# Moving pieces between the 32 steps of a hand-ordered scan loop

## The chip, the cores and the metric

The kernel runs on one core of a Trainium2 chip. The metric is the device time of one execution in microseconds (us), as the median over several executions. Engines are named as in the profile: PE is TensorE (PEld its weight loads), DVE is VectorE, ACT is ScalarE, POOL is GpSimd, and SP is SyncE, which here only issues DMAs.

## The reference, cut to what matters

A batch of 32 sequences of 64 tokens with 512 features passes a conditioning matmul, a Mamba block, an adapter mix and a mixture of experts. The change is within the Mamba part and what is woven into it:

```python
h0 = cond(x, subjects)                    # per-sequence 64x64 matmul + bias
xz = h0 @ in_proj_w.T;  x_, z = split(xz) # 1024 channels each
xc = silu(conv1d(x_, 4 taps))
dt_r, B, C = split(xc @ x_proj_w.T)       # rank 128, 16 states
delta = softplus(dt_r @ dt_proj_w.T + bias)
for t:                                    # 16 states per channel
    h = h * exp(delta_t * A) + (delta_t * xc_t) * B_t
    y_t = (h * C_t).sum(states)
y = (y + xc * D) * silu(z)
x1 = x + y @ out_proj_w.T
x2 = x1 @ W.T + adapters(x1)              # then x1 + experts(x2)
```

## The kernel before, in words

The 2048 tokens are cut into four blocks of 512 (8 sequences each), j = 0 to 3. A block is worked in 32 steps, m = 0 to 31: two halves of the 1024 channels, times 16 states n. Everything is float32. One step treats one state of one half, as four tiles i of 128 channels by 512 tokens:

- ACT makes the decays, `decay` (L927), one 128x504 exponential a tile, into two PSUM buffers.
- POOL makes the inflows, `inflow` (L1194), one product a tile into `dbx`. There is a single `dbx` buffer for each i, so the inflow of step m+1 for tile i has to wait for the scan of step m for tile i.
- DVE runs the recurrence along the tokens, `scan` (L1078), one instruction a tile.
- PE turns the states, `turn_h` (L716), in four tiles t of four 128x128 transposes each, into three PSUM banks. DVE then adds them, weighted with C, into `yacc`, in `add_state` (L1090). It does so one step later, two adds after every two scans. In the first step of a half (n = 0) the sum is started on ACT (L935) instead.

All other work of the layer is cut into named *pieces*, and the list `LINE` says, for each of the 32 steps, which pieces PE issues before it turns tiles 0 to 2 of that step (the first list, "firsts" below) and which between tiles 0 to 2 and tile 3 (the second list, "rests" below). Because the three banks of the transposes are reused, tile 2 of a step cannot be turned before the last add of the step before it, and tile 3 not before the first add of its own step. So the rests of step m run on PE during DVE's step m+1.

The pieces are: `cond` (conditioning, for the next block), `x` and `z` (four 128x512 matmuls each), `silu` and `zsilu` (activation of four tiles of xc or zs, on ACT), `rank` and `bc` (two halves each), `ct` (turns C), `dt` and `ln` (softplus in two parts), `turn` (turns the sums back, halves 0 and 1), `gate` (a product with silu(z) on POOL, one a tile, L1170), `out` (output projection; `out` 2i and 2i+1 fill one bank together), `xr` (turns x1 back), `xa` (adapters), `w` (mixing matmul with one more matmul for the adapter), `row` (turns x2 back), `lg` (router logits), `pre` (first half of the output projection, in the last block only) and `skip` (xc times D). `x`, `cond`, `silu`, `rank`, `bc`, `ct`, `dt0` to `dt3` and `ln0` to `ln3` work for the next block, and are left out in the last one; `out`, `xr`, `xa`, `w`, `row`, `lg`, `turn1` and `gate4` to `gate7` finish the block before, and are left out in block 0.

Every other engine takes its order from the same list:

- ACT empties the banks of step m's pieces in step m+1: firsts after decay i=1, rests after decay i=3. Decay i of a step waits for the scan two tiles earlier.
- DVE does the three convolution instructions of an `x` piece (L981) at the end of step m+1, and the mask product of `xa` (`masked`, L1033) at the end of step m itself, ahead of the convolutions.
- POOL does, after the four inflows of step m, the gates of step m-1, the finish of `ln` of step m-3 (two operations, L1159 and L1162), and the first part of `ln` of step m-2 (two operations, L1152 and L1154).
- SP issues in step m: the row of B for that step (`load_b`, into `b_all`, once POOL has finished the inflows of step m-2), then the weight tiles that take over the slots of the pieces of step m-2 (each waits until the bank of that piece is full), then stores of x1, x2T and x2 rows for pieces two steps back, each waiting for ACT. Near the end of the last block it also loads `res` again, four steps after `xr3`.

PE has only two banks for all pieces but the transposes, used in turn. So a piece waits for the emptying of the last piece but one. The lines that matter most:

```python
for piece in first_at(j, m): piece_of("body", j, piece)
turn_h(j, m, range(0, TURNED))      # TURNED = 3
for piece in rest_at(j, m): piece_of("body", j, piece)
turn_h(j, m, range(TURNED, TB))     # TB = 4
```

Of the kernel before, what the change touches and what calls it, by code (L numbers as in the profile page):

```python
# [41 lines left out]


LINE = [
    (["turn1", "gate4", "gate5"], []),
    (["gate6", "z0"], ["cond0", "gate7"]),
    (["out0"], []),
    (["out1"], ["dt4"]),
    (["out2"], []),
    (["out3"], ["ln4", "cond1"]),  # L50
    (["out4"], []),
    (["out5"], ["dt5"]),
    (["cond2"], ["ln5", "z1"]),
    (["dt6"], ["dt7", "cond3"]),
    (["ln6", "out6"], []),
    (["out7"], []),
    (["xr0", "x0"], ["skip0", "ln7"]),
    (["x1", "z2"], []),
    (["skip1", "xa", "x2"], ["xr1", "xr2"]),
    (["x3"], ["skip2", "skip3"]),  # L60
    (["turn0"], ["x4"]),
    (["silu0"], ["x5", "z3"]),
    (["x6"], ["zsilu0", "x7"]),
    (["w0", "silu1", "rank0"], []),
    (["rank1", "xr3"], ["dt0", "gate0"]),
    (["w1"], ["gate1"]),
    (["gate2", "w2"], ["ln0"]),
    (["w3", "gate3"], ["row0", "dt1"]),
    (["pre0", "bc0"], ["ln1"]),
    (["z4"], ["bc1", "pre1"]),  # L70
    ([], ["lg"]),
    (["dt2"], ["ln2", "pre2", "row1"]),
    (["z5"], ["dt3"]),
    (["z6", "row2"], ["row3"]),
    (["ln3", "pre3", "ct"], ["z7", "zsilu1"]),
    ([], []),
]
ROWS = BATCH + 2 * BB
# [2145 lines left out]
```

How the kernel before makes its waits and increments, by code:

```python
            def load_b(j, m):  # L374
                if m == 0:
                    sp.wait_ge(bt_stored, 16 * (j + 1))
                sp.wait_ge(dbx_made, j * SCANS + HT * (m + 1))
                row = bt_d[bass.ds(j, 1), m % NST, :]
                sp.dma_start(b_all[:, m % RING, :], row.broadcast_to([P, BLK])).then_inc(b_full[m % RING], 16)
# [1 line left out]
            def load_tile(n):  # L382
                section, j, piece = STREAM[n]
                name, i = name_and_number(piece)
                if n >= SLOTS:
                    sp.wait_ge(bank_full, Place(*STREAM[n - SLOTS]).full + 1)
                if name == "x":
                    tile = in_wT[:, :, i * P:(i + 1) * P]
                elif name == "z":
                    tile = in_wT[:, :, DIN + i * P:DIN + (i + 1) * P]
                elif name == "out":
                    tile = out_wT[:, i % 2 * HT:i % 2 * HT + HT, i // 2 * P:(i // 2 + 1) * P]
                elif name in ("pre", "post"):
                    tile = out_wT[:, (HT if name == "post" else 0):(DT if name == "post" else HT), i * P:(i + 1) * P]
                elif name == "xa":
                    tile = mix_d["a_T"]
                else:
                    tile = mix_d["w_T"][:, :, i * P:(i + 1) * P]
                sp.dma_start(wt[:, n % SLOTS], tile).then_inc(wt_full[n % SLOTS], 16)
# [1 line left out]
            def load_res(j):  # L401
                sp.wait_ge(first_x1_stored, 16 * (j - 1))
                sp.wait_ge(x1_stored, 16 * (TB - 1) * (j - 1))
```

## Time and profile before

| | us |
|---|---|
| median of 3 runs | 1880.04 (1879.41 to 1880.5) |
| the profiled execution | 1879.41 |
| its span, first to last instruction | 1877.6 |
| before the loop | 77.5 |
| the four blocks, 77.5 to 1069 | 991.5 |
| what follows | 808.6 |
| DVE busy in the four blocks | 967.1 |
| POOL busy in the four blocks | 806.9 |
| PE busy in the four blocks | 811.4 |

The profiled execution lasted 1879.41 us, 1.8 more than its span. A sum of terms is made against 1879.4. The adds of the last step run on for some microseconds after 1069, and what follows it (output projection of the last half, experts) is not touched by the change.

### The profile page before, as it was taken

Reading aid. Unit: us, or ns where it says so; the run is one execution under the profiler, and the core shown is the slowest. Engines: PE = TensorE matmul, PEld = TensorE weight load, DVE = VectorE, ACT = ScalarE, POOL = GpSimd, SP = SyncE. Lnnn points to the kernel's source line nnn. Section 1 sums busy time; section 2 is a strip of 40 time slices with the busy share of each in tenths; the row PEclk is TensorE's granted clock in tenths of the full one; section 3 lists DMA queues with packets and bytes.
Section 4 is the critical chain, followed back from the end, with each engine's and each line's share of the span. In section 5 each row is a group of like instructions: output and inputs, shape, how many; then the busy total and the mean of one; then the engine's idle time right before and its main releaser. Section 6 shows DMA issues by size and latency. Waiting matters only on the chain. (4 is left out here: it accounts for less than half of the span.)

```text
span 1877.6 us, 28500 instructions
## 1 busy us (share of the span) xinstructions
PE 1646.6 (88%) x7932; PEld 1211.5 (65%) x7932; DVE 1457.8 (78%) x1948; ACT 818.9 (44%) x1220; POOL 1060.1 (56%) x825
## 2 busy tenths in 40 slices
PE   8667868888998998878778999999979999999998
PEld 5255434554455554455445647778879999999997
DVE  3699999999999999999999826677346566565654
ACT  2656665566766667665664411000022233232322
POOL 0289579887599794898977470000044444344433
PEclk9869889999998999989988999999989999999999
DMA  5122112133322322222223342111155656665664
GB/s 128 38 59 68 57 41 76 60 93 81 79 96 85 90 90 68 91 90 62 74 73 112 113 165 70 67 68 44 61 138 127 175 130 172 164 135 141 155 175 70
DMA packets 129895, 182.20 MB, mean 97 GB/s; under 512 B 21379, under 2 KB 79491, under 8 KB 126660
## 3 DMA queue, kind: packets, MB, share of 16 engines
q1 hardware_dynamic: 109540, 131.85, 21.8%
q0 software_dynamic: 17760, 44.05, 12.0%
q10 hardware_dynamic: 2432, 4.33, 0.9%
q8 instruction: 77, 1.26, 0.3%
q14 instruction: 86, 0.70, 0.1%
HBM read 276.45 MB, written 37.36 MB: 167 GB/s over the span
## 5 line engine op out<-in xcount | busy, mean ns | idle before, releaser
L1194 POOL TENSOR_TENSOR arena_kept<-arena_kept,b_all 128x512 f32<-128x512 f32 x512 | 637.0, 1274 | 251.1 <-DVE arena_kept L1078 134.6
L1078 DVE TENSOR_TENSOR_SCAN arena_kept<-da,arena_kept 128x512 f32<-128x512 f32 x512 | 598.5, 1207 | 13.1 <-ACT da L927 8.1
L927 ACT ACTIVATE da<-arena_kept,a_neg 128x504 f32<-128x504 f32 x512 | 347.4, 684 | 244.6 <-DVE arena_kept L1078 238.6
L716 PE MATMUL hT<-ident_kept,arena_kept 128*128 128x128 f32 x2048 | 314.0, 300 | 145.1 <-DVE yacc L1090 88.6
L716 PEld LDWEIGHTS hT<-ident_kept,arena_kept 128*128 128x128 f32 x2048 | 256.4, 154 | 248.2 <-DVE arena_kept L1078 171.6
L1090 DVE SCALAR_TENSOR_TENSOR yacc<-hT,c_now,yacc 128x512 f32<-128x512 f32 x480 | 332.0, 735 | 4.4 <-PE hT L716 4.1
L2078 POOL DMA_INDIRECT out<-y,slots_kept x76 | 139.1, 1831 | 243.3 <-issue 174.4
L516 PE MATMUL bank<-hid,wt 128*128 128x512 f32 x512 | 239.9, 617 | 0.7 <-ACT hid L752 0.7
L516 PEld LDWEIGHTS bank<-hid,wt 128*128 128x128 f32 x512 | 98.8, 202 | 107.3 <-issue 105.7
L1946 ACT ACTIVATE gs<-egp 128x352 f32<-128x352 f32 x73 | 33.8, 464 | 237.5 <-PE eup L1278 236.9
L1714 POOL DMA_DIRECT2D slots_kept<-lists_kept x1 | 0.6, 554 | 222.7 <-DVE lists_kept L1664 222.7
L2073 POOL DMA_INDIRECT xg_kept<-x_scratch,slots_kept x72 | 74.7, 1037 | 68.8 <-ACT y L1985 39.1
L2026 DVE TENSOR_TENSOR a<-gs,eup 128x352 f32<-128x352 f32 x73 | 37.8, 518 | 93.8 <-ACT gs L1946 93.8
L1276 PE MATMUL egp<-w_up_hi_kept,xT_hi 128*128 x292 | 101.0, 346 | 2.9 <-DVE w_up_lo_kept L1270 2.9
L1552 ACT ACTIVATE sgs<-gp 128x512 f32<-128x512 f32 x24 | 14.4, 598 | 196.1 <-PE gp L1278 196.1
L1266 DVE CAST aT_hi<-aT_ps 128x256 fp32r<-128x256 f32 (+1 forms) x144 | 44.4, 350 | 68.4 <-PE aT_ps L1903 68.4
L1277 PE MATMUL egp<-w_up_lo_kept,xT_hi 128*128 x292 | 95.1, 326 | 0.0
L1278 PE MATMUL egp<-w_up_hi_kept,xT_lo 128*128 x292 | 94.8, 325 | 0.0
L1277 PE MATMUL eup<-w_up_lo_kept,xT_hi 128*128 x292 | 94.2, 322 | 0.0
L1276 PE MATMUL eup<-w_up_hi_kept,xT_hi 128*128 x292 | 94.1, 322 | 0.0
L1278 PE MATMUL eup<-w_up_hi_kept,xT_lo 128*128 x292 | 94.1, 322 | 0.0
L1985 ACT ACTIVATE y<-eyp,slots_kept 128x512 f32<-128x512 f32 x72 | 49.5, 687 | 95.6 <-PE eyp L1278 95.6
(234 smaller groups left out, 3186.9 us busy)
## 6 DMA issues: line engine op xcount, KB each, us to landing
w_up_kept<-in_up_T SPq DMA_DIRECT2D x76, 1408.0 KB, 6.1
w_dn_kept<-in_dn_T SPq DMA_DIRECT2D x76, 768.0 KB, 7.4
b_all<-bt_scratch SPq DMA_DIRECT2D x128, 256.0 KB, 3.4
wt<-in_in_T SPq DMA_DIRECT2D x64, 256.0 KB, 3.0
wt<-in_out_T SPq DMA_DIRECT2D x32, 256.0 KB, 2.9
res<-in_x_pad SPq DMA_DIRECT2D x16, 256.0 KB, 3.6
x_scratch<-res SPq DMA_DIRECT2D x16, 256.0 KB, 2.1
wt<-in_w_T SPq DMA_DIRECT2D x16, 256.0 KB, 3.0
```

The costliest lines, as they stand in the source:

```text
L516: mm = nc.tensor.matmul(bank[:], w[:, k, :], hid[:, at.block % RING, k, :], start=(k == 0), stop=(k == KM - 1))
L716: mm = nc.tensor.transpose(turned_in(j, m, t)[:, d * P:(d + 1) * P], h[:, m % RING, d, t * P:(t + 1) * P], ident[:])
L927: nc.scalar.activation(out[:, :, 1:], rows[:, :, 1:], ACT.Exp, scale=a_neg[:, d, n:n + 1]) \
L1078: nc.vector.tensor_tensor_scan(h[:, n % RING, i, :], da[i % RING][:], dbx[:, i, :], 0.0, ALU.mult, ALU.add).then_inc(scan_done, 1)
L1090: nc.vector.scalar_tensor_tensor(out=yacc[:, t, :], in0=turned_in(j, m, t)[:], scalar=scalar, in1=yacc[:, t, :], op0=ALU.mult, op1=ALU.add ...
L1194: nc.gpsimd.tensor_tensor(dbx[:, i, :], u[:, d, :], b_all[:, m % RING, :], ALU.mult) \
L1276: nc.tensor.matmul(out, lhs_hi, rhs_hi, start=first, stop=False)
L1277: nc.tensor.matmul(out, lhs_hi, rhs_lo, start=False, stop=False)
L1278: return nc.tensor.matmul(out, lhs_lo, rhs_hi, start=False, stop=last)
L1985: nc.scalar.mul(y[:, r % YS, :], yp[r % RING][:], slots[:, r, 1:2].bitcast(F32)).then_inc(y_out, 1)
L2073: nc.gpsimd.indirect_dma_start(out=xg[:, s, :], out_offset=None, in_=x2_d, in_offset=bass.IndirectOffsetOnAxis(ap=slots[:, r, 0:1], axis=0)) \
L2078: nc.gpsimd.indirect_dma_start(out=out_d, out_offset=bass.IndirectOffsetOnAxis(ap=slots[:, r % LISTS, 0:1], axis=0), in_=y[:, r % YS, :], ...
```

## The change

Only the list `LINE` changes: the same pieces, each once, stand at other steps or in the other of the two lists. No instruction is added or removed on a compute engine.

```diff
 LINE = [
-    (["turn1", "gate4", "gate5"], []),
-    (["gate6", "z0"], ["cond0", "gate7"]),
-    (["out0"], []),
-    (["out1"], ["dt4"]),
+    (["turn1", "gate4", "gate5"], ["gate6", "gate7"]),
+    (["cond0", "z0"], ["dt4"]),
+    (["out0"], ["cond1"]),
+    (["out1"], []),
     (["out2"], []),
-    (["out3"], ["ln4", "cond1"]),
+    (["ln4", "out3"], ["cond2"]),
     (["out4"], []),
-    (["out5"], ["dt5"]),
-    (["cond2"], ["ln5", "z1"]),
-    (["dt6"], ["dt7", "cond3"]),
-    (["ln6", "out6"], []),
-    (["out7"], []),
-    (["xr0", "x0"], ["skip0", "ln7"]),
-    (["x1", "z2"], []),
-    (["skip1", "xa", "x2"], ["xr1", "xr2"]),
-    (["x3"], ["skip2", "skip3"]),
+    (["out5"], []),
+    (["dt5"], ["z1"]),
+    (["dt6"], ["ln5", "cond3"]),
+    (["out6"], ["ln6"]),
+    (["out7"], ["skip0"]),
+    (["x0"], ["dt7", "ln7"]),
+    (["z2"], ["skip1", "x1", "xr0"]),
+    (["x2", "xr1"], ["skip2"]),
+    (["x3"], ["skip3"]),
     (["turn0"], ["x4"]),
-    (["silu0"], ["x5", "z3"]),
-    (["x6"], ["zsilu0", "x7"]),
-    (["w0", "silu1", "rank0"], []),
-    (["rank1", "xr3"], ["dt0", "gate0"]),
-    (["w1"], ["gate1"]),
-    (["gate2", "w2"], ["ln0"]),
-    (["w3", "gate3"], ["row0", "dt1"]),
-    (["pre0", "bc0"], ["ln1"]),
-    (["z4"], ["bc1", "pre1"]),
-    ([], ["lg"]),
-    (["dt2"], ["ln2", "pre2", "row1"]),
-    (["z5"], ["dt3"]),
-    (["z6", "row2"], ["row3"]),
-    (["ln3", "pre3", "ct"], ["z7", "zsilu1"]),
+    (["silu0", "xa"], ["x5", "z3"]),
+    ([], ["x6", "zsilu0", "x7"]),
+    (["gate0", "w0", "xr2"], ["silu1", "rank0"]),
+    (["rank1"], ["gate1"]),
+    (["xr3", "dt0"], ["ln0", "w1"]),
+    (["gate2", "dt1"], ["w2"]),
+    (["gate3"], ["w3"]),
+    (["bc0", "ln1"], ["pre0"]),
+    (["bc1", "row0"], ["z4"]),
+    ([], ["pre1", "lg"]),
+    (["dt2"], ["z5", "row1"]),
+    (["ln2"], ["z6"]),
+    (["row2", "pre2", "dt3"], ["row3"]),
+    (["ln3", "ct", "z7"], ["pre3", "zsilu1"]),
     ([], []),
 ]
```

The first row of the list is step 0, the last is step 31.

## Rows read from the trace of the kernel before

**Rows 1.** What DVE waited for, 70 to 1080 us: total, times, longest.

```profile
DVE arena_kept L1078 <- ACT da L927: 8.1, 13, 1.3
DVE conv_sum L981 <- ACT conv_sum L769: 4.3, 6, 0.7
DVE yacc L1090 <- PE hT L716: 4.1, 4, 1.7
```

**Rows 2.** Windows: busy time by engine, PE's granted clock; blocks 1 and 3.

```profile
327.00:573.00 246.00, 213.13 (x981) 130.73 (x980) 239.94 (x275) 160.76 (x246) 201.20 (x163) 0.97 0.29 83
...
819.00:1069.00 250.00, 203.37 (x939) 131.96 (x938) 242.16 (x273) 139.49 (x215) 202.47 (x164) 0.90 0.27 85
```

**Rows 3.** Timeline of DVE, block 1, steps 11 and 12: start, length, instructions.

```profile
413.45 2.33 DVE L1078 TENSOR_TENSOR_SCAN arena_kept<-da,arena_kept 128x512 f32<-128x512 f32 x2
...
416.99 2.33 DVE L1078 TENSOR_TENSOR_SCAN arena_kept<-da,arena_kept 128x512 f32<-128x512 f32 x2
```

**Rows 4.** Timeline, end of block 0 and start of block 1 (scan at 332.64).

```profile
327.35 1.28 ACT L783 ACT_TABLE_LOAD   x1
...
328.64 1.91 ACT L783 ACTIVATE arena_kept<-arena_kept 128x2048 f32<-128x2048 f32 x1
...
332.64 2.34 DVE L1078 TENSOR_TENSOR_SCAN arena_kept<-da,arena_kept 128x512 f32<-128x512 f32 x2 [1.16 <-POOL arena_kept L1194]
```

**Rows 5.** Timeline of POOL from block 0's step 31 to block 1's step 2.

```profile
317.49 4.95 POOL L1194 TENSOR_TENSOR arena_kept<-arena_kept,b_all 128x512 f32<-128x512 f32 x4
...
327.68 4.97 POOL L1194 TENSOR_TENSOR arena_kept<-arena_kept,b_all 128x512 f32<-128x512 f32 x4
...
339.71 2.49 POOL L1170 TENSOR_TENSOR skip<-skip,arena_kept 128x512 f32<-128x512 f32 x2
342.17 4.97 POOL L1194 TENSOR_TENSOR arena_kept<-arena_kept,b_all 128x512 f32<-128x512 f32 x4
```

**Rows 6.** Timeline of all engines there: five scans, steps 1 and 2.

```profile
340.91 5.93 DVE L1078 TENSOR_TENSOR_SCAN arena_kept<-da,arena_kept 128x512 f32<-128x512 f32 x5 [0.20 <-ACT da L927]
```

**Rows 7.** Timeline of PE, block 1, steps 16 and 17.

```profile
464.17 3.68 PE L516 MATMUL bank<-hid,wt 128*128 128x512 f32 x8
467.69 0.60 PE L716 MATMUL hT<-ident_kept,arena_kept 128*128 128x128 f32 x4
```

**Rows 8.** Timeline of DVE, block 1, steps 17 to 20.

```profile
464.84 4.56 DVE L1078 TENSOR_TENSOR_SCAN arena_kept<-da,arena_kept 128x512 f32<-128x512 f32 x4
470.09 1.54 DVE L981 SCALAR_TENSOR_TENSOR conv_sum<-xpad,ch,conv_sum 128x512 f32<-128x512 f32 x2 [0.69 <-ACT conv_sum L769]
...
476.51 2.34 DVE L1078 TENSOR_TENSOR_SCAN arena_kept<-da,arena_kept 128x512 f32<-128x512 f32 x2 [0.55 <-ACT da L927]
...
499.40 1.22 DVE L1078 TENSOR_TENSOR_SCAN arena_kept<-da,arena_kept 128x512 f32<-128x512 f32 x1 [1.06 <-ACT da L927]
```

**Rows 9.** Groups on DVE, 327 to 1069 us: the mask product of `xa`.

```profile
L1033 DVE TENSOR_TENSOR x_sb<-bank,mask 128x512 f32<-128x512 f32 x3 | 2.1, 692 | 0.4
```

**Rows 10.** Timeline of PE, block 3, steps 26 to 28: `lg`, then `pre2`.

```profile
1033.99 3.64 PE L664 MATMUL bank<-gate_T,x2T 128*128 128x16 f32 x32
...
1041.90 4.95 PE L604 MATMUL bank<-skip,wt 128*128 128x512 f32 x8
1046.68 1.05 PE L607 MATMUL bank<-ident_kept,res 128*128 128x128 f32 x8
```

**Rows 11.** Timeline of DVE there; the add that waited.

```profile
1048.65 0.75 DVE L1090 SCALAR_TENSOR_TENSOR yacc<-hT,c_now,yacc 128x512 f32<-128x512 f32 x1 [1.69 <-PE hT L716]
```

**Rows 12.** Windows, PE alone: the stretch after `lg`; busy, granted clock.

```profile
1038.00:1045.00 7.00, 6.02 (x19) 0.53 0.00 0
```

**Rows 13.** DMA issues in 1000 to 1030 us: count, KB, median us to landing.

```profile
b_all<-bt_scratch SPq DMA_DIRECT2D x4, 256.0 KB, 4.1
...
x2T_scratch<-x2T SPq DMA_DIRECT2D x1, 1024.0 KB, 5.1
```

**Rows 14.** Timeline of DVE, block 1, start of step 5.

```profile
366.05 2.43 DVE L1078 TENSOR_TENSOR_SCAN arena_kept<-da,arena_kept 128x512 f32<-128x512 f32 x2 [0.16 <-POOL arena_kept L1194]
```

## The prediction, made before the changed kernel ran

> **What bounds the kernel now.** I read the windows first. In block 1 DVE is busy 239.9 of 246.0 us, POOL 201.2 and PE 213.1; block 3 has 242.2 of 250.0 on DVE [rows 2]. The timeline of DVE shows what full use looks like: two scans and two adds every 3.54 us, so 7.09 us for a plain step [rows 3]. So the scan engine is the bound, and the loop can only lose or regain DVE's idle time. That idle is small: 991.5 less 967.1 busy is 24.4 us over four blocks. Of this, 8.1 us wait for a decay, 4.3 for the convolution's input and 4.1 for transposes [rows 1]. An order of pieces can win some of it, and can add more where a queue that now keeps pace falls behind. The question is thus, step by step, which queue is late after the move. Times below are relative to the start T of DVE's step.
>
> A plain step leaves PE this room: tiles 0 to 2 of the step before end about T+0.5, tile 3 must be ready by about T+6.4. A piece of eight records takes 3.6 us [rows 7], in use 3.5 because neighbours overlap; rests therefore have about 5.4 us, one large piece and a little.
>
> **The change part by part.**
>
> *Block changeover, POOL.* Before, `zsilu1` held ACT for 1.28 + 1.91 + 1.28 = 4.5 us from 327.35, and the first scan of block 1 began at 332.64 after 1.16 us idle [rows 4]. The row names POOL, whose fourth inflow ended late, but scan 0 needs only the first one, and the decay could start only at about 331.85. `z7` is now a first, so ACT starts `zsilu1` about T+3.0 of step 31 and the decay is early. That alone gives back some 1.0 us at each of three changeovers. But POOL gets more work in the same stretch. `ln2` moves a step later, so its two finishing operations come after the inflows of step 31; and all four gates 4 to 7 come after the inflows of step 1, where two were. From the end of step 31's inflows to the first inflow of step 2 POOL now has 6 softplus operations, 8 inflows, 4 gates and one inflow. Four softplus operations took 5.24 us (from the end of one group of inflows, 317.49 + 4.95, to the next at 327.68), four inflows 4.97, two gates 2.49 [rows 5]: 7.9 + 9.9 + 5.0 + 1.25 = 24.0 us. Before, step 31's inflows ended at 322.4. Two softplus operations ahead of them drop away (2.6 us), part of which turns into waiting for scans; of 0 to 2.6 I take 1.1, end 321.3. Then step 2's first scan starts at 345.3. Before, it was the fifth of the five that began at 340.91, at 344.5 [rows 6]. So a changeover costs +0.8, and in the next two, where POOL ends the inflows 0.3 us later against DVE, some +1.3. Term: +3.5 us for three. Bounds: if POOL is early enough, DVE sets the time and only the 1.0 us each remain, -2.9; if nothing drops away ahead, +1.9 each, +6.
>
> *`xa` from step 14 to step 17, blocks 1 and 2.* Its mask product (0.69 us [rows 9], 0.84 with the gap) leaves step 14. In step 17, a short one of four scans, DVE reaches the product at 469.40, and waited until 470.09 for convolution input [rows 8]. PE finishes `x4` and tile 3 at about 468.3 [rows 7], then needs 3.5 us for `xa`: 471.9. DVE waits 2.5, multiplies (0.61 until the next starts), and does the same three convolutions (2.24). Step 18 starts at 474.8 instead of 472.3, +2.5. Less 0.84, and less 0.65 since `silu0`'s hold of ACT, which costs a 0.55 us wait [rows 8], is now hidden by the later DVE: +1.0 each. Term: +2.0. Bounds: -1.7 (if `xa` were ready in time and 0.65 hidden as well) to +5.
>
> *`silu1` from firsts to rests of step 19.* It holds ACT another 4.5 us by the durations of rows 4, now from T+3.05 to T+7.6 of step 20; the next step's decay is there at T+8.3 against 7.09. A stall of 1.2 us takes the place of the one of 1.06 (1.16 over the step) [rows 8]; in block 0 it was about 0.6. Term: +0.6. Here a rule of the Trainium skill can be weighed: the page "ScalarE: Activation LUTs", section "What ACT_TABLE_LOAD costs", has about 2.66 us for each switch of tables, most of the excess a drain. The rows show 1.28 us with the activation following 0.01 us later, and by the page's figure each such hold would be an estimated 7.2 us and this stall nearly 4 us. The measurement decides, and the sum uses 4.5 us.
>
> `rank1` now waits for `silu1` about 2.2 us longer while PE idles. At full clock it still fits; at half clock the turned tile is up to 1.5 us late, in each of three blocks. PE fell to nearly half clock in other thin stretches (0.53 granted in 7 us after `lg`, at 6.0 us busy [rows 12]). 0 to 4.5, I take 1.5, as the gap is shorter than the empty stretches.
>
> *Block 3.* `pre1` and `lg` now stand together in the rests of step 26. `lg` takes 3.64 us, a `pre` 3.6 and 1.05 for its residual [rows 7, 10], overlapped together 7.8. From T+0.5 they end at 8.3, the fourth tile at 8.8, so DVE stalls 2.5 us. Before, `pre2` ran cold, 4.95 us [rows 10], and DVE waited 1.69 [rows 11] and 0.7 in steps 28 and 29, more than half of its 4.1 us of waiting for transposes [rows 1]. That goes, but `z5` and `pre3` take a similar place with perhaps 1.0. Net +1.0. Next, `w3` as a rest ends about T+4.9 of step 24. SP's weight tile behind it, four `res` loads (0.63 us of issue each) and the 1 MB store of x2T now all precede the row of B for step 26. It is issued at about T+8.9, and 4.1 to 5.1 us of landing [rows 13] puts it at T+13 to T+14; with 1.25 of inflow that is 0.1 to 1.1 past its step's start at 14.2. With the shorter lead for `pre0`'s residual, +1.0. Steps 17 to 22: `xa` about 1.1 of wait, cold `w0` and `w1` some 1.8, against 2.8 before: 0. Term: +2.0, bounds -2 to +6.
>
> *The rest.* Steps 13 and 14 lose small waits, -0.4. A cold `z5` as a rest in block 0 costs +0.3, and the chain `w1`, `w2`, `w3`, `bc0` in steps 21 to 25 fills PE to within 0.1 us of its room, +0.4. The late row of B in steps 4 to 9 stays, since the tile behind an even `out` still waits for the odd one. `cond`, `dt`, `ln5`, `skip`, `xr` and `row` fit under DVE where they land, cost nothing, and would cost about their PE time (0.5 to 1.9 us) without that cover. Term: +0.3, bounds -2 to +3.
>
> **Sum:** 3.5 + 2.0 + 0.6 + 1.5 + 2.0 + 0.3 = +9.9 us on 1879.4 gives 1889.3; I say 1889. The profiled execution is 0.6 us under the median, well within what the estimate can tell.
>
> **The rivals.**
>
> *POOL is not the limiter (not slower).* POOL is busy 82% of block 1 [rows 2], so it could have the slack. If the first inflow of step 2 is ready within 22.4 us of the start of step 31, the gates cost nothing. Then the changeovers bring -2.9 instead of +3.5, and a POOL that is not behind would also regain the small delays of steps 4 to 9, such as the 0.16 of [rows 14]; the lengths of those steps are 3.8 us over 7.09 each, summed over blocks 1 to 3: 9.9 - 6.4 - 3.8 = -0.3, 1879. Against it: the queue is strictly in order, and my count of 19 operations needs 24.0. Chance 0.12; with errors of the other terms this is also where nearly all of "faster" lies.
>
> *PE stays at full clock.* The new order puts large pieces nearer each other. Then the cold parts vanish: 1.5 for `rank1`, 0.3, and in block 3 the 2.8 for `w0`, `w1`, `z5` and `pre3`: 9.9 - 4.6 = +5.3, 1884.7. For it: block 1 is granted 0.97 already; against: block 3 only 0.90 [rows 2]. Chance 0.25.
>
> *PE goes cold more often.* Rests have a deadline that firsts have less of. A large piece at half clock takes about 7 us, 1.5 to 2 us over the room. If `rank1` (3), `z5` (4) and the `w` rests (2 or 3) are hit by 1 us more each, +8 to +9: 1898. Chance 0.15.
>
> *Forecast,* 1889, between 1885 and 1893: chance 0.48.
>
> **How the numbers follow.** A change of 0.2% (3.8 us) is about what a measurement of this kernel can tell. Faster than 1876.3 needs nearly all of the lower bounds: 0.07. Within 0.2%, most of the first rival and some of the second: 0.16. Slower: 0.77. The range 1880.5 to 1897 leaves the first rival's lower half and the far end of the third.
>
> **What would show it.** In the changed profile: no wait of about 1 us at the first scan of blocks 1 to 3, but DVE waiting about 2 us for POOL at step 2; in step 17 of blocks 1 and 2 the mask product waiting 2.5 us for PE (L640); after `silu1` a wait of 1.2 for the decay; in block 3 an add of step 27 waiting 2.5 us behind `lg`. The prediction is wrong if POOL finishes the gates before DVE needs step 2, or if the clock of block 3 moves far from 0.90. It also fails if a wait in SP's queue that I count as hidden delays the row of B in blocks 1 and 2.

## The result: slower, and by two and a half times the predicted amount

| | before | after |
|---|---|---|
| median, us | 1880.27 | 1907.02 |
| profiled execution, us | 1879.41 | 1908.14 |
| its span, us | 1877.6 | 1906.3 |
| the four blocks, DVE's first scan to its last step, us | 987.0 | 1016.7 |

The ratio of the times is 1.0135, 95% interval 1.0119 to 1.0151, which is +25.4 us on 1880. One of the four timed executions of the changed kernel took 2764 us at a granted clock of 0.55; it is left out of the ratio but not of the median of 1907.02, which would be 1905.5 without it. The others lie between 1904.6 and 1908.5. The forecast was 1889, within a range of 1880.5 to 1897, so +9.9 us. The sign was right, size and range were not. No compute work was added, so the loss must be idle time of DVE. The windows over the four blocks, as long as each now lasts (busy time of PE, PEld, DVE, ACT, POOL, then PE's granted clock), answer to [rows 2]:

```profile
77.00:338.00 261.00, 186.64 (x782) 115.59 (x783) 249.72 (x287) 158.80 (x240) 205.96 (x166) 0.82 0.18 57
338.00:596.00 258.00, 225.93 (x1005) 135.81 (x1002) 247.64 (x285) 163.12 (x251) 208.85 (x170) 0.95 0.27 83
596.00:859.00 263.00, 231.92 (x998) 139.15 (x997) 247.41 (x284) 162.99 (x251) 208.25 (x169) 0.92 0.26 81
859.00:1094.00 235.00, 187.64 (x840) 120.48 (x839) 220.11 (x246) 124.22 (x195) 184.49 (x149) 0.89 0.26 78
```

DVE is busy 964.9 us of them (962.6 before, up to the start of the same last step), and idle 52.1 instead of 24.4. What it waited for, 70 to 1080 us (total, times, longest), against [rows 1]:

```profile
DVE yacc L1090 <- PE hT L716: 21.9, 15, 5.2
DVE arena_kept L1078 <- POOL arena_kept L1194: 9.8, 16, 2.2
DVE x_sb L1033 <- PE bank L640: 6.2, 3, 2.7
DVE arena_kept L1078 <- issue: 4.7, 4, 1.2
DVE conv_sum L981 <- ACT conv_sum L769: 3.2, 4, 1.0
DVE arena_kept L1078 <- ACT da L927: 2.7, 6, 1.3
```

The waits for a decay, where the new order was to gain, shrank by less than from 8.1 to 2.7: three of the four waits listed under "issue" are the decay behind `silu1` in step 21, and that row had 1.2 before. Taken together the two rows fell from 9.3 to 7.4. The waits for turned tiles grew from 4.1 to 21.9, and new ones stand for POOL's inflows and for `xa`. The length of each DVE step (first scan to next first scan) shows where. The sum of the differences over the blocks is +29.7, of which the head and the tail give back 1.0, so the span grew by 28.7. That is this one execution, among the longer ones; over all of them the loss is 25.4.

| term | predicted | measured | from the steps |
|---|---|---|---|
| changeovers | +3.5 | +8.2 | step 1: +1.54, +1.53, +1.51; step 31: +0.32, +1.60, +1.66 |
| `xa` | +2.0 | +1.7 | step 17: +2.05, +2.60; step 14: -0.84 twice; step 18: -0.65 twice |
| `silu1` | +0.6 | +0.85 | step 20: +0.63, +0.11, +0.11 |
| `rank1` | +1.5 | +5.2 | step 21: +2.18, +0.01, +2.99 |
| block 3 | +2.0 | +7.0 | step 25 +2.90, 27 +5.27, 28 -1.57, 29 -0.84, 17 and 18 +1.1, the others +0.1 |
| the rest | +0.3 | +6.9 | block 0: steps 2, 13, 15 +1.09, +0.43, +0.94; block 2: 6, 28 +1.37, +1.06; small ones |

**A changeover.** The timeline of PE, DVE and ACT at the end of block 1:

```profile
580.31 6.65 PE L516 MATMUL bank<-hid,wt 128*128 128x512 f32 x8
...
587.44 1.41 DVE L1090 SCALAR_TENSOR_TENSOR yacc<-hT,c_now,yacc 128x512 f32<-128x512 f32 x2 [2.64 <-PE hT L716]
...
593.31 1.29 ACT L927 ACTIVATE da<-arena_kept,a_neg 128x504 f32<-128x504 f32 x2
```

`z7`, now a first, ran at half clock (0.55 granted): 6.65 us for its eight records. Eight such records take 3.68 in [rows 7], and `z7` itself, as a rest, took 4.61 here before, at 0.78 granted. The adds waited 2.64 for the tiles behind it. The decay (593.31) did come before the scan of the new block (595.58), as forecast, and that scan waited for nothing; but `z7` took more than the 1.0 us this was to bring. A step later, POOL and DVE:

```profile
599.70 1.26 POOL L1194 TENSOR_TENSOR arena_kept<-arena_kept,b_all 128x512 f32<-128x512 f32 x1 [0.27 <-DVE arena_kept L1078]
601.41 1.28 POOL L1194 TENSOR_TENSOR arena_kept<-arena_kept,b_all 128x512 f32<-128x512 f32 x1 [0.45 <-DVE arena_kept L1078]
602.65 4.97 POOL L1170 TENSOR_TENSOR skip<-skip,arena_kept 128x512 f32<-128x512 f32 x4
607.55 4.97 POOL L1194 TENSOR_TENSOR arena_kept<-arena_kept,b_all 128x512 f32<-128x512 f32 x4
...
608.97 2.42 DVE L1078 TENSOR_TENSOR_SCAN arena_kept<-da,arena_kept 128x512 f32<-128x512 f32 x2 [1.55 <-POOL arena_kept L1194]
```

The last two inflows of step 1 waited for scans: POOL had caught up with DVE during step 0. In this kernel its delay begins there and not in step 31. The last inflow of step 1 starts at 601.41. From there POOL needs 1.24 us until the gates, 4.90 for them and 1.42 until the scan of step 2, together 7.56. DVE was ready for that scan after 6.01.

**`silu1` and `rank1`.** Block 2, steps 20 and 21, against [rows 8]:

```profile
764.55 1.28 ACT L775 ACT_TABLE_LOAD   x1
...
767.81 6.77 PE L527 MATMUL bank<-arena_kept,w_xp 128*128 128x512 f32 x8 [2.58 <-ACT arena_kept L775]
...
769.07 1.29 ACT L927 ACTIVATE da<-arena_kept,a_neg 128x504 f32<-128x504 f32 x2
769.84 2.34 DVE L1078 TENSOR_TENSOR_SCAN arena_kept<-da,arena_kept 128x512 f32<-128x512 f32 x2 [1.18 <-issue]
775.05 1.41 DVE L1090 SCALAR_TENSOR_TENSOR yacc<-hT,c_now,yacc 128x512 f32<-128x512 f32 x2 [2.87 <-PE hT L716]
```

T is 761.49: ACT is held from T+3.06 to T+7.58 and the scan starts at T+8.35, as the prediction had it to the tenth. Then PE, empty for 2.58 us, runs `rank1` at half clock (0.54 granted), and DVE waits 2.87.

**`xa`** in block 1, beside [rows 9]: the mask product waited 2.14 (2.5 was forecast).

```profile
478.10 0.69 DVE L1033 TENSOR_TENSOR x_sb<-bank,mask 128x512 f32<-128x512 f32 x1 [2.14 <-PE bank L640]
```

**Block 3,** steps 25 to 27, against [rows 10] and [rows 11]:

```profile
1042.91 0.44 SPq L380 DMA_DIRECT2D b_all<-bt_scratch  x1
1047.47 1.16 PE L607 MATMUL bank<-ident_kept,res 128*128 128x128 f32 x8 [1.22 <-DMA res<-in_x_pad]
1050.61 12.43 POOL L1194 TENSOR_TENSOR arena_kept<-arena_kept,b_all 128x512 f32<-128x512 f32 x10 [7.26 <-DMA b_all<-bt_scratch]
1052.01 2.42 DVE L1078 TENSOR_TENSOR_SCAN arena_kept<-da,arena_kept 128x512 f32<-128x512 f32 x2 [2.15 <-POOL arena_kept L1194]
...
1058.03 2.82 PE L716 MATMUL hT<-ident_kept,arena_kept 128*128 128x128 f32 x12 [2.19 <-DVE arena_kept L1078]
1060.64 5.34 PE L604 MATMUL bank<-skip,wt 128*128 128x512 f32 x8
1065.82 1.05 PE L607 MATMUL bank<-ident_kept,res 128*128 128x128 f32 x8
1066.71 3.64 PE L664 MATMUL bank<-gate_T,x2T 128*128 128x16 f32 x32
1070.88 0.75 DVE L1090 SCALAR_TENSOR_TENSOR yacc<-hT,c_now,yacc 128x512 f32<-128x512 f32 x1 [5.17 <-PE hT L716]
```

The row of B, issued behind four `res` loads and the 1 MB store of x2T, landed after 7.6 us, and the first inflow started 7.7 us after the issue. The rows of B in [rows 13] have a median of 4.1 (the 5.1 there is the store). And `pre1` with `lg` did stall an add, but for 5.17 us: the twelve transposes ahead of them took 2.82 (1.96 at full clock) at 0.50 granted, and `pre1` 5.34 (3.60) at 0.67. Steps 17 and 18, which the forecast put at 0 for this block, are 1.1 longer together, from the wait of `xa`.

### The profile page after: what moved, and what is told of

Read it like the earlier page. It is cut to its first block and busy times, and to the rows that moved or that the text cites. A ratio compares the mean times of both kernels' runs of the same rounds, so it can differ in the third digit from the quotient of the medians.

```text
span 1906.3 us, 28500 instructions
## 1 busy us (share of the span) xinstructions
PE 1668.7 (88%) x7932; PEld 1217.0 (64%) x7932; DVE 1460.1 (77%) x1948; ACT 816.5 (43%) x1220; POOL 1054.8 (55%) x825
## 3 DMA queue, kind: packets, MB, share of 16 engines
q0 software_dynamic: 17760, 44.05, 11.6%
## 5 line engine op out<-in xcount | busy, mean ns | idle before, releaser
L716 PE MATMUL hT<-ident_kept,arena_kept 128*128 128x128 f32 x2048 | 322.8, 303 | 149.9 <-DVE yacc L1090 78.4
L2078 POOL DMA_INDIRECT out<-y,slots_kept x76 | 131.6, 1732 | 252.9 <-issue 160.1
L516 PE MATMUL bank<-hid,wt 128*128 128x512 f32 x512 | 246.0, 630 | 4.0 <-ACT conv_sum L769 3.3
L1552 ACT ACTIVATE sgs<-gp 128x512 f32<-128x512 f32 x24 | 14.4, 598 | 196.7 <-PE gp L1278 196.7
```

The lines of the kernel that those rows point to most:

```text
L516: mm = nc.tensor.matmul(bank[:], w[:, k, :], hid[:, at.block % RING, k, :], start=(k == 0), stop=(k == KM - 1))
L716: mm = nc.tensor.transpose(turned_in(j, m, t)[:, d * P:(d + 1) * P], h[:, m % RING, d, t * P:(t + 1) * P], ident[:])
L2078: nc.gpsimd.indirect_dma_start(out=out_d, out_offset=bass.IndirectOffsetOnAxis(ap=slots[:, r % LISTS, 0:1], axis=0), in_=y[:, r % YS, :], ...
```

## The experiments

Sixteen kernels ran. Each has its median and, where timed in rounds, the ratio to the kernel before with its 95% interval. Where a difference in us is given for a whole kernel, it is that ratio on 1880 us, so that it is taken against the kernel before of the same rounds; each has an interval of 2 to 4 us either way. Step lengths are from the profiled execution. In the edits that repeat transposes, the values computed stay the same.

### One move undone in the changed kernel

Four runs: the gates, then `silu1` and `rank0`, then `pre1`, then `z7`.

```diff
-    (["turn1", "gate4", "gate5"], ["gate6", "gate7"]),
-    (["cond0", "z0"], ["dt4"]),
+    (["turn1", "gate4", "gate5"], []),
+    (["gate6", "cond0", "z0"], ["dt4", "gate7"]),
...
-    (["gate0", "w0", "xr2"], ["silu1", "rank0"]),
+    (["gate0", "w0", "xr2", "silu1", "rank0"], []),
...
-    ([], ["pre1", "lg"]),
+    (["pre1"], ["lg"]),
...
-    (["ln3", "ct", "z7"], ["pre3", "zsilu1"]),
+    (["ln3", "pre3", "ct"], ["z7", "zsilu1"]),
```

> The changed kernel, with gate6 back as a first and gate7 back as a rest of step 1; all else as changed. Theory A (the four gates in a row on POOL hold back the first inflow of step 2, and nothing else depends on them): the waits of 1.55 us of DVE for POOL at the first scan of step 2 in blocks 1 to 3 vanish, -4.6 us in all. Theory B (POOL's whole chain from step 31 on sets the time, as the prediction had it): with two gates fewer POOL is only 2.5 us further ahead, and the first scan of blocks 1 to 3 starts earlier as well, -6 us or more. Theory C (the time is given back later): no change within 1 us.

> The changed kernel, with silu1 and rank0 back among the firsts of step 19; all else as changed. Theory A (PE idles before rank1 for silu1, its clock falls, and rank1 at half clock makes the turned tile late): the waits of 2.06 and 2.87 us of DVE for transposes in step 21 of blocks 0 and 2 vanish, block 1 stays, step 20 gains some 0.1 to 0.6, together -5 to -6.5 us. Theory B (the stall comes from rank1 standing there as such): step 21 of blocks 0 and 2 stays about 2 to 3 us long, under -1.5 us in all.

> The changed kernel, with pre1 as a first of step 26 and only lg as a rest; pre1 exists in block 3 alone, so blocks 0 to 2 are not touched. Theory A (pre1 and lg in one rest are too long for the room before the fourth tile): step 27 of block 3 falls from 12.4 to about 7.1 us, but a clock that falls after lg costs 1 to 2 us later in steps 28 and 29, -3 to -5.3 us. Theory B (the late row of B of step 25 leaves PE and POOL behind, and that is paid wherever): step 27 stays over 9 us, under -2 us in all.

> The changed kernel, with the last working step as before: ln3, pre3, ct as firsts and z7, zsilu1 as rests of step 30. Theory A (z7 as a first runs at half clock and makes the turned tile of step 31 late by 2.7 us, which is more than the 1.0 us that the hidden zsilu1 gives): steps 31 of blocks 1 and 2 fall from 13.1 to about 11.5 us, block 0 by 0.3 to 0.5, block 3 by 0.5: -3.5 us. Theory B (POOL is the limiter at the changeover): POOL's chain is as long as before the edit, so the first scan of step 2 stays where it is, within 1 us.

They gave 1903.62 (1.0125, 1.0107 to 1.0144), 1905.61 (1.0141, 1.0124 to 1.0158), 1902.08 (1.0130, 1.0107 to 1.0153) and 1908.11 (1.0147, 1.0127 to 1.0167). That is +23.5, +26.5, +24.4 and +27.6 us, where the changed kernel has +25.4: no move undone by itself gives back anything clear of the noise. Yet at their places three of the moves did what was expected. Without the gates' move step 1 is 5.00 again in blocks 1 and 2; without that of `silu1`, step 21 is 7.09 in all blocks; with `pre1` first, step 27 of block 3 falls from 12.36 to 8.24 (7.1 was expected). With `z7` back, theory A held only in part: step 31 fell to 11.80 and 12.26 in blocks 1 and 2 (13.10 and 13.15 after), but rose from 12.03 to 12.31 in block 0. What was saved came back elsewhere: with the gates undone, step 2 of blocks 1 to 3 took 8.16, 7.68 and 7.38 (7.18 and 7.19 after); with `silu1` undone, step 2 of block 1 took 10.76 and step 31 of block 0 13.26.

Part of this is no effect of an edit at all. `pre1` is left out in blocks 0 to 2, so with it put back these blocks run the same instructions as in the changed kernel. Yet they took 777.5 us against 781.8, and step 21 of block 2, 10.08 there, was 7.10. A reading of single steps from one execution of these orders can be off by that much: the `rank1` term of the table would be +2.2 in that execution.

### Six moves undone together

The four above, and `xa` and `w3` back as firsts of steps 14 and 23.

> The changed kernel with all six moves undone together: gate6 and gate7, silu1 and rank0, pre1 from the rest with lg, z7 and zsilu1, xa back to step 14, and w3 as a first. The other moves stay (dt, ln, cond, xr, x, z, row, bc). Theory A (these six and the clock that they let fall are the cause of nearly all): 1880 to 1884. Theory B (the clock falls anyway, since the other moves thin out PE's work elsewhere): the single undos gave 0 to 4 us each and do not add up, so it stays over 1890.

It gave 1901.34, ratio 1.0117 (1.0094 to 1.0139), +22.0 us: theory A fell. That is not the price of the moves left in it alone, since pieces put back now stand beside pieces that stayed moved. With `xa` back in step 14, behind `x1` and `xr0` in the rests of step 13, step 14 of blocks 1 and 2 takes 12.07 and 13.76 (9.33 after, 10.17 before), 5.5 us more than before. With `w3` back as a first of step 23, step 24 of blocks 1 to 3 takes 8.07, 8.07 and 7.91 (7.09 before and after), another 2.8; of the sixteen kernels only the two with `w3` back show this. The rest is spread over many steps, most of them of 7.6 to 8.7 instead of some 7.1.

### Transposes repeated, so that PE is not empty

Tile 3 of step 19 (ahead of the wait for `silu1`), then also tile 2 of step 29 (ahead of `z7`), in the changed kernel:

```diff
+            AGAIN = {(19, 3): 5, (29, 2): 5}
...
-                    for d in range(HT):
+                    for d in [d for again in range(AGAIN.get((m, t), 1)) for d in range(HT)]:
```

> The changed kernel with nothing moved: in step 19 PE turns the fourth tile five times over instead of once (16 more 128x128 transposes that write the same values again, 1.8 us at full clock), so that it idles less before rank1. No work is left out. Theory A (the clock falls in PE's idle before rank1): the extra work costs nothing, as it ends before DVE needs the tile, and step 21 is 7.1 us in every block instead of 9.27 and 10.08 in blocks 0 and 2. Theory B (transposes do not hold the clock, or the clock is not the cause): step 21 stays at 9 to 10 us in blocks 0 and 2, and step 20 may grow by up to 1 us.

> The same repeats in step 19, and in step 29 the third tile turned five times over as well, in the light stretch ahead of ct and z7. Nothing moved, nothing left out. Theory A (the clock is what makes z7 as a first too long): step 31 falls to 10.5 us in blocks 0 to 2 instead of 12.0, 13.1 and 13.15, one microsecond under the 11.5 of the kernel before, since zsilu1 is hidden there; with step 21 the time falls by 10 to 12 us against the changed kernel. Theory B (z7 as a first is too long by itself): step 31 stays over 12 us.

With the first alone (one execution) 1897.45, span 1895.6; with both 1898.18, ratio 1.0099 (1.0082 to 1.0116). Block 2, steps 20 and 21, with the first alone:

```profile
763.91 3.70 PE L527 MATMUL bank<-arena_kept,w_xp 128*128 128x512 f32 x8 [0.84 <-ACT arena_kept L777]
...
765.94 2.34 DVE L1080 TENSOR_TENSOR_SCAN arena_kept<-da,arena_kept 128x512 f32<-128x512 f32 x2 [1.19 <-issue]
768.20 1.38 DVE L1092 SCALAR_TENSOR_TENSOR yacc<-hT,c_now,yacc 128x512 f32<-128x512 f32 x2
```

Here T is 757.58, so `rank1` starts at T+6.33, as in the changed kernel (T+6.32). It takes 3.70 at 1.00 granted instead of 6.77 at 0.54, and the add does not wait. Step 21 is 7.59, 7.10, 7.10 in the three blocks, from 9.27, 7.10, 10.08. So what the move of `silu1` cost at `rank1` is PE's half clock (in block 0, where `rank1` still began at half clock and took 4.07, 0.5 is left). With the stretch ahead of `z7` filled too, `z7` takes 3.70 and step 31 falls to 10.82, 11.08, 11.13 (from 12.03, 13.10, 13.15). The run with both places is 6.8 us under the changed kernel. How much of it each place brings is open: the run with the first alone, a single execution, was no slower.

The run with both places also shows POOL's queue at the changeover with `z7` at full clock. From block 2 to block 3:

```profile
834.37 4.96 POOL L1196 TENSOR_TENSOR arena_kept<-arena_kept,b_all 128x512 f32<-128x512 f32 x4
...
847.14 9.86 POOL L1196 TENSOR_TENSOR arena_kept<-arena_kept,b_all 128x512 f32<-128x512 f32 x8
856.96 4.96 POOL L1172 TENSOR_TENSOR skip<-skip,arena_kept 128x512 f32<-128x512 f32 x4
861.88 3.72 POOL L1196 TENSOR_TENSOR arena_kept<-arena_kept,b_all 128x512 f32<-128x512 f32 x3
863.28 2.43 DVE L1080 TENSOR_TENSOR_SCAN arena_kept<-da,arena_kept 128x512 f32<-128x512 f32 x2 [1.82 <-POOL arena_kept L1196]
```

The eight inflows of steps 0 and 1 now run without one wait for a scan. From the end of step 31's inflows (839.3) to the end of step 2's first one (863.1) the 19 operations take 23.8 us; the prediction had counted 24.0. Steps 31, 0 and 1 are together 0.9, 1.4 and 1.4 us longer than before at the three changeovers (1.8, 3.1 and 3.2 in the changed kernel); the prediction had 0.8, 1.3 and 1.3.

Then a list with 27 entries, wherever PE seemed to have room:

> The changed kernel with transposes repeated at many thin places, so that PE has fewer empty stretches: tile 3 of step 19 and tile 2 of step 29 five times, tile 3 of steps 3, 4 and 7 three times, in block 0 tile 3 of steps 1, 2, 5, 6, 8, 10, 11 five times and of 14, 15, 22, 23 three times, in block 3 tile 3 of steps 11 to 16 and 25 five times, of 17, 18, 20 three times and tile 0 of step 26 three times. The values computed stay the same. Theory A (the half clock is what makes the new order slow): half-clock time in the loop falls from 215 us to under 150, the waits for transposes (22.3 us) to under 8, and the time to 1886 to 1893; what stays is the gates (4.5), xa (1.9), silu1 (0.9) and the late row of B in block 3. Theory B (the order itself is the cause, or the repeated work costs as much as it saves): 1896 or more.

It gave 1909.10, ratio 1.0157 (1.0137 to 1.0177). Theory A held in one number only: time at half clock in the blocks fell from 215 to 130 us, blocks 0 and 3 are granted 0.90 and 0.94 instead of 0.82 and 0.89. The time did not follow, and the waits for transposes only fell to 14.4, not to under 8. Repeated tiles ended late themselves; in step 15 of block 3 PE's 52 transposes took 7.74 us (0.81 granted), and DVE waited twice:

```profile
963.04 7.74 PE L718 MATMUL hT<-ident_kept,arena_kept 128*128 128x128 f32 x52 [2.75 <-DVE yacc L1092]
...
970.82 0.75 DVE L1092 SCALAR_TENSOR_TENSOR yacc<-hT,c_now,yacc 128x512 f32<-128x512 f32 x1 [1.24 <-PE hT L718]
```

Blocks 1 and 2, with few repeats, took 255.9 and 256.4, like the run with two places (257.2 and 255.5), against 252.9 and 252.6 before. So filling PE in this way was worth about 7 us at best and not the whole loss. What a full clock without the added work would bring, no run shows.

### The best repairs together

Gates 6 and 7, `pre1` and `w3` back, with the two places repeated.

> The changed kernel with gate6 back in the firsts of step 1 and gate7 in its rests, pre1 back as a first of step 26, w3 back as a first of step 23, and the fourth tile of step 19 and the third of step 29 turned five times. Theory A (gains add where the clock is held: 3.4 for the gates, 4.9 for pre1, 8.8 for the repeats): 1888 to 1892. Theory B (a stall that is removed comes back elsewhere, at another phase of the clock): 1895 to 1900.

It gave 1895.96, ratio 1.0088 (1.0065 to 1.0112), 8.8 us under the changed kernel and not the 17 of theory A. But the gains that theory A added up (3.4, 4.9 and 8.8) were differences of medians from the 1907.02, which is too high, and from different rounds. By the ratios they are 1.9, 0.9 and 6.8, and 9.6 together: the gains do add up within the noise, and they are small. New stalls are there all the same. The `w3` put back costs 2.8 in steps 24, as above. Step 4 of block 1 was now 8.63 (7.35 after). POOL waited there for a row of B that SP issued at 365.31, 2.9 us into the step (1.6 in the changed kernel), and that landed 4.3 us later:

```profile
365.31 0.63 SPq L380 DMA_DIRECT2D b_all<-bt_scratch  x1
...
369.68 2.50 POOL L1196 TENSOR_TENSOR arena_kept<-arena_kept,b_all 128x512 f32<-128x512 f32 x2 [6.73 <-DMA b_all<-bt_scratch]
```

### Five moves alone in the kernel before

The gates, `silu1` with `rank0`, `xa`, `pre1` beside `lg`, and `z7` ahead of `pre3`, with all else as before.

> The kernel before with five single moves of the change made alone: all gates 6 and 7 in the rests of step 0, silu1 and rank0 in the rests of step 19, xa in the firsts of step 17, pre1 beside lg in the rests of step 26, z7 and zsilu1 as first (pre3 as rest) of step 30. Theory A (each move has a price of its own, and the other moves, which the prediction costed at about +0.3, carry the rest): undoing these and the w move gave back 6 us of 27, so making them costs about 6, 1884 to 1888, with step 17 of blocks 1 and 2 about 2 us longer, step 1 1.5 us longer, step 27 of block 3 3 to 5 longer. Theory B (these five carry most of the loss, and undoing them failed only because other stalls took their place): 1895 to 1902, with new stalls of step 21 too.

It gave 1898.30, ratio 1.0095 (1.0073 to 1.0117): 18 us, where theory A, from the undone ones, had some 6. It fell, and theory B held. Of the 25.4 us, some 7.5 are thus left for all other moves, with an interval of some 5 either way. The steps are those of the changed kernel: step 1 is 6.53 three times, step 21 is 9.33, 9.03 and 10.41, step 17 of blocks 1 and 2 10.54 and 9.90, step 27 of block 3 12.09.

### Each move alone in the kernel before

```diff
-    (["turn1", "gate4", "gate5"], []),
-    (["gate6", "z0"], ["cond0", "gate7"]),
+    (["turn1", "gate4", "gate5"], ["gate6", "gate7"]),
+    (["z0"], ["cond0"]),
```

> The kernel before with gates 6 and 7 both in the rests of step 0 and nothing else moved (step 1: z0 as first, cond0 as rest). Theory A (own price): step 1 of blocks 1 to 3 becomes 6.5 instead of 5.0, the rest stays, +4.6, 1883 to 1886. Theory B (a stall removed or added shifts the others, and little is left of it): within 2 of the kernel before. The prediction's account, by which POOL is late since all 19 of its operations from step 31 on are in a row, would here have the 1.55 us wait too, but no less of it than in the changed kernel only if POOL's lead is used up within steps 0 and 1.

1887.66, ratio 1.0040 (1.0027 to 1.0054), +7.5. Step 1 is 6.54 in all three blocks, with step 31 as before (11.60 against 11.50 in block 1):

```profile
337.15 1.28 POOL L1194 TENSOR_TENSOR arena_kept<-arena_kept,b_all 128x512 f32<-128x512 f32 x1 [0.44 <-DVE arena_kept L1078]
338.38 4.96 POOL L1170 TENSOR_TENSOR skip<-skip,arena_kept 128x512 f32<-128x512 f32 x4
343.30 4.97 POOL L1194 TENSOR_TENSOR arena_kept<-arena_kept,b_all 128x512 f32<-128x512 f32 x4
...
344.71 2.42 DVE L1078 TENSOR_TENSOR_SCAN arena_kept<-da,arena_kept 128x512 f32<-128x512 f32 x2 [1.55 <-POOL arena_kept L1194]
```

The same 0.44, 4.96 and 1.55 as in the changed kernel, though step 31 is 11.6 here and 13.1 there. At three changeovers that is 4.6 us; new stalls at step 6 of blocks 1 and 2 (8.23 and 8.86, from 7.40 and 7.09) are another 2.6.

```diff
-    (["w0", "silu1", "rank0"], []),
+    (["w0"], ["silu1", "rank0"]),
```

> The kernel before with silu1 and rank0 in the rests of step 19 and nothing else moved. Theory A: steps 20 longer by 0.6, 0.1, 0.1 and step 21 by 2 to 3 in each of blocks 0 to 2, since rank1 as first of step 20 runs after an empty stretch at half clock: +6 to +9, 1886 to 1889. Theory B (rank1 is cold only with the other moves): step 21 stays 7.1, +1, 1881.

1891.14, ratio 1.0058 (1.0041 to 1.0074), +10.9. Step 21 is 9.23, 9.15 and 10.01, the last by

```profile
760.03 6.26 PE L527 MATMUL bank<-arena_kept,w_xp 128*128 128x512 f32 x8 [2.58 <-ACT arena_kept L775]
...
767.20 1.41 DVE L1090 SCALAR_TENSOR_TENSOR yacc<-hT,c_now,yacc 128x512 f32<-128x512 f32 x2 [2.81 <-PE hT L716]
```

It is the costliest of the moves; step 21 brings 7.1. (The profiled execution, 1886.8, was the fastest of four.)

```diff
-    (["z4"], ["bc1", "pre1"]),
-    ([], ["lg"]),
+    (["z4"], ["bc1"]),
+    ([], ["pre1", "lg"]),
```

> The kernel before with pre1 beside lg in the rests of step 26 and nothing else moved. Theory A: step 27 of block 3 about 12.2 instead of 7.1, step 28 about 0.7 shorter: +3 to +4.5, 1883 to 1885. Theory B: with the clock of the kernel before the two pieces end 2.5 late as the prediction had it, less what pre2 gives back: +1.0, 1881.

1883.83, ratio 1.0021 (1.0011 to 1.0030), +3.9. Step 27 of block 3 is 12.09 from 7.09, step 28 8.39 from 9.07.

```diff
-    (["skip1", "xa", "x2"], ["xr1", "xr2"]),
+    (["skip1", "x2"], ["xr1", "xr2"]),
...
-    (["silu0"], ["x5", "z3"]),
+    (["silu0", "xa"], ["x5", "z3"]),
```

> The kernel before with xa in the firsts of step 17 instead of step 14 and nothing else moved. Theory A (own price): step 17 of blocks 1 and 2 longer by 2.1 to 3.0 and of block 3 by 1.6 to 1.9, steps 14 and 18 shorter by 0.84 and 0.65: about +1, +1 and +0.3 by block, +2.3 to +3, 1882 to 1883. Theory B: other stalls come in, as clocks shift: +5 or more.

1883.80, ratio 1.0018 (1.0008 to 1.0029), +3.4. Step 17 is 10.72, 10.03 and 7.17 in blocks 1 to 3, from 7.50, 7.53 and 5.00; steps 14 and 18 fall as forecast.

The four add up to +25.8, more than the five of the run above (+18). Each of the four has a price of its own, clear of the noise, and together they cost less than the sum; why, no run shows.

### A faster version?

`z7` alone was to gain, if it stays at full clock, in the kernel before; then with `pre2` moved too:

```diff
-    (["ln3", "pre3", "ct"], ["z7", "zsilu1"]),
+    (["ln3", "ct", "z7"], ["pre3", "zsilu1"]),
...
+            AGAIN = {(29, 2): 5}
```

> The kernel before, with two edits: the last working step as in the changed kernel (ln3, ct, z7 as firsts; pre3, zsilu1 as rests), and the third tile of step 29 turned five times over, to keep PE busy ahead of z7. Theory A (zsilu1's hold of ACT costs 1.0 us a changeover and the clock is all that stands against moving it): steps 31 of blocks 0 to 2 fall from 11.7, 11.5, 11.5 to 10.5 us, and the time by 3 us, to about 1877. Theory B: POOL's chain is the limit at the changeover, so what step 31 wins is lost in steps 1 and 2: no change.

> The kernel before with z7 and zsilu1 ahead of pre3, the third tile of step 29 turned five times, and pre2 in the firsts of step 27 instead of its rests. Theory A (pre2 was late in block 3 since it ran at half clock in the rests after lg; as a first it has more time): steps 28 and 29 of block 3 shrink from 9.07 and 7.94 to 7.5 and 7.1, 2.4 us, 1876 to 1878. Theory B (it waits for the bank, or a later piece is late in its place): 1879 to 1882.

1879.28, ratio 1.0004 (0.9992 to 1.0016), and 1878.94, ratio 0.9999 (0.9988 to 1.0010). Both do at their place what was expected. Step 31 falls by 0.9 to 1.1 to 10.58, 10.59, 10.58 in the first; in the second, steps 28 and 29 of block 3 fall from 9.07 and 7.94 to 7.33 and 7.09. Neither moves the time: steps 6 of block 1 (8.38, from 7.40) and 11 of block 2 (8.10, from 7.09) are longer in the first, steps 6 of blocks 1 and 2 (8.45 and 8.84) in the second, and the part after the blocks is 1.5 and 2.5 us longer. No version faster than the kernel before was found.

The gain in step 31 is not the place of `z7`, though. In the kernel before, `z7` as a rest took 4.88, 4.61 and 4.64 us in blocks 0 to 2, partly at half clock, and so delayed `zsilu1`. In the run with the move of `silu1` alone `z7` is the same rest, but at 1.00 granted in blocks 1 and 2. In block 1, PE and ACT, step 31 starting at 580.08:

```profile
580.58 3.60 PE L516 MATMUL bank<-hid,wt 128*128 128x512 f32 x8
...
584.82 1.28 ACT L783 ACT_TABLE_LOAD   x1
...
589.34 1.29 ACT L927 ACTIVATE da<-arena_kept,a_neg 128x504 f32<-128x504 f32 x2
```

Step 31 is 10.59 and 10.54 in these two blocks, as short as with `z7` moved, the tile repeated and `z7` at 3.70. The 1.0 us a changeover that the move was to bring is what `z7` at full clock brings at its old place. Why the clock stayed up there, no run shows.

## Why the prediction was wrong, step by step

*Right.* The bound (DVE, losing only through idle time), the sign, and the two terms that rest on counting one engine's queue at full clock: `xa` (+1.7 for +2.0) and the hold of `silu1` (+0.85 for +0.6). Two more holds of ACT measured 4.5 us again (588.79 to 593.31, 764.55 to 769.07). The 2.66 us for a table switch (the Trainium skill, "ScalarE: Activation LUTs", "What ACT_TABLE_LOAD costs") is not seen here: each load takes 1.28 and the next activation starts 0.01 to 0.02 us later.

*`rank1`: the step that failed is "at half clock the turned tile is up to 1.5 us late", "0 to 4.5, I take 1.5".* At full clock the piece just fits (with the transposes repeated, its tile is ready as DVE asks), so at half clock nearly the whole 3.1 us that it takes more become waiting: 2.2 to 3.0 in a block. The bound of 1.5 a block was half of that, and the value taken supposed that a 2.6 us gap would mostly leave the clock up. It went down in two of three blocks, and in all three when the move stood alone. Shown, by the move alone (+2.1 to +2.9 in step 21) and by the repeated transposes that took it away: with them `rank1` takes 3.70 in blocks 1 and 2 of all four kernels that have them, without them in 5 of 12 such places.

*Changeover: the step that failed is that the move of `z7` itself was put at nothing but a gain ("`z7` is now a first, so ACT starts `zsilu1` about T+3.0 of step 31").* As a first it took 5.4, 6.7 and 6.4 us in blocks 0 to 2, `zsilu1` started at T+4.6, 6.3 and 6.3, and step 31 grew by 0.3, 1.6 and 1.6 instead of shrinking by 1.0. The chain of 19 operations, "the queue is strictly in order, and my count of 19 operations needs 24.0", was not what set the time in the changed kernel: DVE was late enough for POOL to catch up in step 0, its inflows waited 0.27 and 0.45 for scans, and the four gates cost 1.5 from the last inflow of step 1 on. Two costs of about equal size, +8.2 together, stand where +3.5 was forecast. With `z7` at full clock the forecast comes true in all its parts: `zsilu1` starts at T+3.06, the 19 operations take 23.8 without a wait, and the changeovers cost 0.9 + 1.4 + 1.4 = 3.7. So the count was right for a clock that PE did not have here. That the gates cost 1.5 also without the longer chain is shown by their move alone, where POOL has two softplus operations fewer; and in the run with five moves, which lacks them too, the one changeover with `z7` at full clock costs 0.6.

*Block 3: "from T+0.5 they end at 8.3 [...] so DVE stalls 2.5 us" had the right place, and its durations were those of full clock.* Transposes and `pre1` at 0.50 and 0.67 of the clock take 2.6 more, and the stall is 5.17; alone, the move costs 3.9. "4.1 to 5.1 us of landing" was mis-sized: the 5.1 of [rows 13] is the landing of the x2T store, and this row of B took 7.6. Step 25 grew by 2.9 where 1.0 was taken. In the kernel before, a row of B issued right behind the same four `res` loads, but ahead of the store, landed after 5.0 us. So the load of the store is the likelier cause; that is read from the order of issue, not tried. That the move of `w3` is behind it is shown: with `w3` back as a first the same burst is issued 2.5 us earlier in the step. Its row of B still takes 7.1 us with six moves undone, and 8.1 in the other such run, but step 25 is 7.09 and 8.11, at the price of 0.8 in step 24.

*The rest: "cost nothing" was wrong.* The pieces that fit under DVE by their PE time brought +6.9 here, and the run with the five moves made alone leaves some 7.5 for them and `w3`. In block 0 steps 2, 13 and 15 grew; step 2 does so in every kernel that has the new order of `cond0` and `z0`, and in none of the others. Which of the small moves brings how much is open: `w3` and `xa` alone undone, and the moves of `dt`, `ln` and `cond`, were not run, and why step 2 grows is not shown.

*The rivals.* POOL was the limiter at step 2, so the first one fell. The second (full clock) was the reverse of what happened: time at half clock in the blocks rose from 174 to 215 us. The third, PE cold more often, named the mechanism and put 1898 on it, at a chance of 0.15; it was nearest, and still some 7 us short. Of the 25.4 us, the repeated tiles at two places give back 6.8; the gates stand for 4.6, the late row of B for 2.9. The rest is not attributed piece by piece.

## What to carry to other kernels

When a piece is moved so that it follows a gap on PE, cost it at half clock in full, and ask whether it had any slack at full clock: without slack the whole difference is paid. In a queue with single buffers, a count of operations holds only from the last place where it waited for its consumer, and a delay of the consumer (here 1.6 us by `z7`) moves that place. In a loop balanced to a few tenths of a microsecond, price a move by making it alone in the old kernel: undone in the new one, none of four showed anything clear of the noise, while four made alone cost 3 to 11 us. Before a gain is put down to a piece's new place, look whether a run has the same gain with the piece at its old place: the 1.0 us of `z7` was its clock. And compare by the ratio within the same rounds: medians of different rounds suggested gains of 3.4 and 4.9 us where the ratios have 1.9 and 0.9.

## What was not expected of the hardware

- The same gap of 2.58 us on PE ahead of `rank1` stands 18 times in the six kernels that have this move and no repeated tile. In 13 of them `rank1` took 5.2 to 6.8 us (0.54 granted for 6.77), in 5 it took 3.70 at full clock, as in block 1 of the changed kernel. The same order can thus cost 0 or 3 us. Even the same instructions do not settle which: with `pre1` put back, which touches block 3 alone, block 2 had 3.70 for 6.77.
- Repeated 128x128 float32 transposes kept PE at full clock here: with 16 more of them ahead of the gap `rank1` ran at 1.00 granted in blocks 1 and 2, and the list with 27 entries brought the half-clock time from 215 to 130 us.
- `lg`, 32 matmuls with 16 columns each, takes 3.64 us [rows 10], as long as 8 records of 512 columns, and a stretch partly at half clock follows it: 0.53 granted before [rows 12], and after the change 0.63 granted, with 2.95 us for the sixteen transposes behind it (2.16 in the last step of block 1).
